# Softmax sums by one-column products in a score bank, and three moves of row splits, in an attention and expert kernel

## The chip, the cores and the metric

The kernel runs on one core of one Trainium2 chip. The metric is device time in microseconds (us). Before the change it is 1903.29 us, the median of 3 runs (1898.18 to 1903.45). The engines are called as the profile calls them: PE is TensorE, DVE is VectorE, ACT is ScalarE, POOL is GpSimd, SP is SyncE (which issues all DMAs here).

## The reference

A block of cross attention is followed by a block of routed experts. The change is in the attention. `x` has 16 batches of 56 tokens of 256 numbers, the context 16 batches of 1500 keys; there are 16 heads of 128. Cut to what matters:

```python
q = rms_norm(x @ q_w + q_b, nq_s).reshape(B, S, H, D)
k_txt = rms_norm(txt_ctx @ k_w + k_b, nkt_s)   # 1243 keys a batch
k_img = rms_norm(img_ctx @ ki_w + ki_b, nki_s) # 257 keys a batch
attn = softmax(einsum('bshd,blhd->bhsl', q, k) / sqrt(D))
out = einsum('bhsl,blhd->bshd', attn, v)       # once for text, once for image
x = x + (out_txt + out_img).reshape(B, S, INNER) @ o_w + o_b
```

The two softmaxes are separate. Each needs, for every token and head, the sum of its exponentials over its keys; the reciprocal of this sum scales the average of the values.

## The kernel before, in words

The kernel has five stages, one after the other: a prologue with a layer norm, the projection of the queries (`project`), the attention (`attend`), the outputs (`outputs`) and the experts (`experts`). `project` folds the key weights into the queries, so that `attend` multiplies the raw context with "absorbed queries" of 256 numbers per token and head, 896 columns a batch, worked on as two halves of 448 columns.

All fp32 products are made from two parts: a value is split into a high part (fp32r) and the rest, and three products (high by high, high by rest, rest by high) stand for one.

`attend` loops over 16 batches (`batches`, L951: the first, a loop, the last, and a tail). A batch has 13 tiles of up to 128 keys: tiles 0 to 2 are the image, tiles 3 to 12 the text. Tile 2 holds a single key and is called `LONE`. A unit `u` is one tile and one half, so a batch has 26 units (`UNITS`), and the code of every engine is written out as 26 steps. The order on each engine is the order of the code, with semaphores between the engines; nothing is planned at run time.

What one step does, engine by engine:

- **PE** (`body_of`, L1252): the score products of unit `step` into one of three PSUM banks (`scores`, L1178: six products of 448 columns; for the single key two products of prepared terms, L1190); at steps 3, 5 (text, of the batch before) and 9, 11 (image) two products that add up a finished sum over the partitions (`sums`, L1227, into the bank `GRAM`); on even steps five products for the norm of the next tile (`gram`, L1173); then six products of the average of unit `step - 2` (`average`, L1210; none for the single key). The averages of the last two units follow in steps 0 and 1 of the next batch (`carried`).
- **ACT** (`body`, L1373): the exponential of unit `step - 1`, twice, once as high part `p_high` and once in full into the score bank (`exponentials`, L1332); on even steps the high part of a tile two ahead (`prepare`, L1316); at some steps a high part of the absorbed queries (`split_u` at 1, 3 and 10, 12), of the single key's terms (`split_lone` at 14, 16), a copy of the finished text averages (`copy_o`), and at steps 4, 6, 10, 12 a copy of a finished sum row (`copy_sum`, L1357).
- **DVE** (`body`, L1526): `take` (L1516) of unit `step - 1`: the rest `p_low` of the exponential (`split_probs`), the add to the running sum `p_sum` (`add`, L1471; for the single key a row of one partition), and the seed, a copy of the query biases into the bank just read, which the scores three units later add onto (`seed`, L1430). On even steps `norm` (L1445), the mean square of a tile's keys; at steps 2, 4, 6, 8 and 10 it stands ahead of the `take` (`norms_first`, L1531). `split_sum` (L1483) splits a finished sum in two operations, at steps 1, 2 (text) and 7, 8 (image). `reciprocals` (L1504) at steps 10 (text) and 16 (image).
- **POOL** (`body`, L1701): on even steps `key_root` (L1628, the inverse root of the norm), on odd steps `split_tile` (`c_low`, the rest of a tile, natural and transposed, 512 numbers a partition) and `twice` (`c_twice`, an operand of the norm); beside these one longer operation in nearly every even step (`scale_u`, `split_u`, `scale_o`), and at steps 17 and 19 `split_lone`, the rest of the single key's terms.
- **SP** (`body_of`, L1081): one tile load per tile, and at certain tiles (`set_end`, L1059) the loads and stores of the batch's ends. A finished sum goes from a row in SBUF to DRAM (`store_sums`), back as columns of 112 partitions by 8 (`load_sums`), gets its reciprocal on DVE, goes to DRAM again (`store_reciprocals`) and comes back spread over all partitions (`load_reciprocals`), where POOL scales the averages (`scale_o`).

The score banks take turns by `u % 3`; unit 0 of a batch uses the bank of unit 24 of the batch before. The order of DVE around a unit:

```python
def take(it, u, has_next):
    if u // 2 == LONE:
        dve.wait_ge(exp_done, UNITS * it + u + 1 + CREDIT["exp_done"])
        seed_after(it, u, has_next)
    split_probs(it, u)
    add(it, u)
    if u // 2 != LONE and (has_next or u + SC_RING < UNITS):
        dve.wait_ge(sum_added, UNITS * it + u + 1 + CREDIT["sum_added"])
        seed_after(it, u, has_next)
```

A layer norm (`layer_norm`, L117) runs in the prologue and ahead of the experts; its L142 makes fp32 products of 112 stationary columns with one moving column. The prologue's `ones` is used there.

Of the kernel before, what the change touches and what calls it, by code (L numbers as in the profile page):

```python
# [49 lines left out]
AVERAGES = UNITS - 2  # L50
TOK = 112
# [25 lines left out]
          "sum_split": 4, "stage_used": TILES, "o_copied": 2, "recip_ready": 2, "o_scaled": 4, "norm_summed": 3,  # L77
          "lone_split": 2, "max_tile_done": 1, "sum_wide": 2, "sum_copied": 1, "max_scores": 1, "max_listed": 16, "sums_stored": 32,
# [17 lines left out]
def averaged(u):  # L96

    return u + 1 - min(max(u + 1 - 2 * LONE, 0), 2)

# [81 lines left out]
def build(nc, xT_in, ctx_in, lone_in, qw_in, kw_in, kwb_in, vw_in, small_in, router_in, bias_in, ffn_in, out):  # L181
    ctx = ExitStack()
    with ctx:
# [15 lines left out]
        with attn:  # L199
# [19 lines left out]
            with proj:  # L219
# [10 lines left out]
                spent = attend(nc, ctx_in, lone_in, qw_in, kw_in, psum, ident, minus_half, zeros, small, key_scale, *by_head,  # L230
# [189 lines left out]
def project(nc, qw_in, kw_in, psum, ident, minus_half, zeros, small, key_scale, bias_high, bias_low, x_high, x_low,  # L420
# [4 lines left out]
    with ctx:  # L425
# [112 lines left out]
        def tensor(pe):  # L538
# [262 lines left out]
def attend(nc, ctx_in, lone_in, qw_in, kw_in, psum, ident, minus_half, zeros, small, key_scale, bias_high, bias_low, x_high,  # L801
# [4 lines left out]
    with ctx:  # L806
# [18 lines left out]
        sum_cols, recip_cols = sb("sum_cols", [TOK, 2, NTOK]), sb("recip_cols", [TOK, 2, NTOK])  # L825
# [44 lines left out]
        def first_low(gp):  # L870
# [21 lines left out]
        p_sum_high, p_sum_low = sb("p_sum_high", [P, 2, HALF], F32R), sb("p_sum_low", [P, 2, HALF], F32R)  # L892
        sum_row = sb("sum_row", [1, 4, HALF])
# [13 lines left out]
        sums_dram = nc.dram_tensor("sums", [2 * B, HS], F32, kind="Internal").ap()  # L907
# [31 lines left out]
        sum_added, sum_high_ready, sum_split, sum_wide, sum_copied = (  # L939
            sem("sum_added"), sem("sum_high_ready"), sem("sum_split"), sem("sum_wide"), sem("sum_copied"))  # L940
        sums_stored, sums_loaded, recip_ready, recip_stored, recip_loaded = (
            sem("sums_stored"), sem("sums_loaded"), sem("recip_ready"), sem("recip_stored"), sem("recip_loaded"))
# [22 lines left out]
        def bank_of(u):  # L965
            return SC + u % SC_RING

# [5 lines left out]
        def _(sp):  # L973
# [24 lines left out]
            def store_sums(it, s):  # L998
                sp.wait_ge(sum_copied, 4 * it + 2 * s + 2 + CREDIT["sum_copied"])
                sp.dma_start(sums_dram[ds(2 * it + s, 1), :], sum_row[0:1, 2 * s:2 * s + 2, :]  # L1000
                             .rearrange("o a n -> o (a n)")).then_inc(sums_stored, 16)

            def load_sums(it, s):
                sp.wait_ge(sums_stored, 16 * (2 * it + s + 1) + CREDIT["sums_stored"])
                sp.wait_ge(recip_ready, 2 * it + s - 1 + CREDIT["recip_ready"])
                sp.dma_start(sum_cols[:, s, :], sums_dram[ds(2 * it + s, 1), :].rearrange("a (p i) -> p (a i)", i=NTOK))\
                    .then_inc(sums_loaded, 16)

            def store_reciprocals(it, s):
                sp.wait_ge(recip_ready, 2 * it + s + 1 + CREDIT["recip_ready"])  # L1010
                sp.dma_start(recip_dram[ds(2 * it + s, 1), :].rearrange("a (p i) -> p (a i)", i=NTOK),
                             recip_cols[:, s, :]).then_inc(recip_stored, 16)
# [105 lines left out]
            def tail(it):  # L1118
                store_o(it - 1, IMAGE)
                store_sums(it - 1, TEXT)  # L1120
                load_sums(it - 1, TEXT)
# [7 lines left out]
            sp.sem_inc(sums_stored, CREDIT["sums_stored"])  # L1129
# [24 lines left out]
        def _(pe):  # L1154
            pe.sem_inc(scores_done, CREDIT["scores_done"])
            pe.sem_inc(av_done, CREDIT["av_done"])
            pe.sem_inc(sum_wide, CREDIT["sum_wide"])
# [20 lines left out]
            def scores(it, u, safe):  # L1178
# [20 lines left out]
                if not safe:  # L1199
# [27 lines left out]
            def sums(it, s, half, grams):  # L1227

# [1110 lines left out]
```

## Time and profile before

| what | us |
|---|---|
| median of 3 runs | 1903.29 |
| lowest, highest | 1898.18, 1903.45 |
| the profiled execution | 1903.73 |
| its span, first to last instruction | 1902.0 |
| mean granted clock of TensorE | 0.971 of full |
| POOL busy | 1204.3 |
| DVE busy | 1397.3 |
| ACT busy | 985.9 |

The attention fills the span from about 233 to 1447 us. A row of the timeline gives the start, the duration, engine, line, operation, the program's names (out <- in), the shapes and how many instructions it merges; in brackets stands the idle time of the engine just before it and what ended it. Instructions on one engine overlap a little, so a start may come before the end of the one before. Matmuls are pipelined: one of 448 columns lasts 0.37 us, and the next starts some 0.2 us after it. A line can be that of a helper: L1424 is every subtraction on DVE, L1314 every plain copy on ACT.

### The profile page before, as it was taken

What the parts mean: (1) busy time and instruction counts of PE and PEld (TensorE: products, weight loads), DVE (VectorE), ACT (ScalarE), POOL (GpSimd) and SP (SyncE); (2) the same over time, 40 slices, a digit from 0 to 9 for tenths busy, and PEclk for the clock granted to TensorE, in tenths of its full rate; (3) what the DMA queues carried; (4) which work ended last, traced back from release to release, by engine and by line L of the source; (5) the groups of instructions that cost most, each with busy time, mean ns of one, the idle gap of its engine ahead of it and who ended that gap; (6) DMA issues with size and microseconds to landing.
All of it is one profiled execution on the core that took longest, in us unless ns stands there. A gap on an engine that the chain in (4) does not pass through costs nothing. (4 is left out here: it accounts for less than half of the span.)

```text
span 1902.0 us, 30825 instructions
## 1 busy us (share of the span) xinstructions
PE 1733.7 (91%) x8731; PEld 1541.6 (81%) x8731; DVE 1397.3 (73%) x2577; ACT 985.9 (52%) x1657; POOL 1204.3 (63%) x1053
## 2 busy tenths in 40 slices
PE   7899889999999999999999999999992998699998
PEld 6677778888889889888888898898891886588887
DVE  4444587887887887978878878879772664577776
ACT  3455455565555555655655565556552563244443
POOL 1333588878878888788788798798862231133332
PEclk9999899999999999999999999999996999799999
DMA  3366554566556465554565564564436782133332
GB/s 110 127 239 232 175 164 104 114 123 137 115 118 131 108 117 123 121 120 113 128 132 118 120 134 103 116 128 123 95 92 203 249 267 88 66 109 118 114 115 74
DMA packets 417365, 251.20 MB, mean 132 GB/s; under 512 B 350272, under 2 KB 368832, under 8 KB 415520
## 3 DMA queue, kind: packets, MB, share of 16 engines
q1 hardware_dynamic: 417312, 250.55, 51.5%
q8 instruction: 26, 0.43, 0.1%
q14 instruction: 27, 0.22, 0.0%
HBM read 187.71 MB, written 60.10 MB: 130 GB/s over the span
## 5 line engine op out<-in xcount | busy, mean ns | idle before, releaser
L1341 ACT ACTIVATE p_high<-psum,key_rms 128x448 fp32r<-128x448 f32 x384 | 244.8, 638 | 397.1 <-PE psum L1164 396.9
L1162 PE MATMUL psum<-p_high,c_high 128*128 128x448 f32 (+1 forms) x768 | 287.8, 375 | 48.2 <-DVE p_low L1424 48.2
L1424 DVE TENSOR_TENSOR p_low<-psum,p_high 128x448 fp32r<-128x448 f32 x384 | 236.3, 615 | 96.6 <-ACT psum L1343 95.7
L1162 PE MATMUL psum<-u_high,c_high 128*128 128x448 f32 x768 | 285.9, 372 | 20.2 <-DVE psum L1435 14.1
L1163 PE MATMUL psum<-u_low,c_high 128*128 128x448 f32 x768 | 282.9, 368 | 0.0
L1164 PE MATMUL psum<-u_high,c_low 128*128 128x448 f32 x768 | 281.8, 367 | 0.0
L1164 PE MATMUL psum<-p_high,c_low 128*128 128x448 f32 (+1 forms) x768 | 281.4, 366 | 0.0
L1163 PE MATMUL psum<-p_low,c_high 128*128 128x448 f32 (+1 forms) x768 | 281.0, 366 | 0.0
L1636 POOL TENSOR_TENSOR c_low<-stage,c_high 128x512 fp32r<-128x512 f32 x208 | 274.7, 1321 | 0.0
L1435 DVE COPY psum<-beta_wide 128x448 f32<-128x448 f32 x416 | 259.4, 627 | 20.3 <-DMA beta_wide<-absorbed_biases 4.5
L1630 POOL TENSOR_TENSOR key_rms<-key_ms,minus_half 128x1 f32<-128x1 f32 x209 | 119.4, 571 | 188.4 <-DVE key_ms L1449 183.4
L1343 ACT ACTIVATE psum<-psum,key_rms 128x448 f32<-128x448 f32 x384 | 232.5, 606 | 0.0
L1162 PEld LDWEIGHTS psum<-p_high,c_high 128*128 128x128 f32 (+1 forms) x768 | 144.0, 188 | 72.9 <-DVE p_low L1424 62.2
L1480 DVE TENSOR_TENSOR p_sum<-psum,p_sum 128x448 f32<-128x448 f32 (+1 forms) x320 | 196.2, 613 | 0.0
L1162 PEld LDWEIGHTS psum<-u_high,c_high 128*128 128x128 f32 x768 | 144.9, 189 | 44.8 <-DVE psum L1435 20.7
L2043 POOL TENSOR_TENSOR scaled_gate<-gated,p_wide 128x448 f32<-128x448 f32 x64 | 83.7, 1308 | 154.0 <-ACT gated L2144 150.5
L1649 POOL TENSOR_TENSOR c_twice<-stage,c_low 128x256 f32<-128x256 f32 x208 | 169.9, 817 | 16.4 <-POOL c_low L1636 2.4
L1449 DVE CUSTOM_DVE_ANT_0 junk<-psum,c_twice 128x257 bf16<-128x257 f32 x208 | 88.6, 426 | 92.2 <-POOL c_twice L1649 90.3
L1164 PEld LDWEIGHTS psum<-u_high,c_low 128*128 128x128 f32 x768 | 145.2, 189 | 12.7
L1163 PEld LDWEIGHTS psum<-u_low,c_high 128*128 128x128 f32 x768 | 145.2, 189 | 10.9
L1164 PEld LDWEIGHTS psum<-p_high,c_low 128*128 128x128 f32 (+1 forms) x768 | 144.1, 188 | 12.1
L1163 PEld LDWEIGHTS psum<-p_low,c_high 128*128 128x128 f32 (+1 forms) x768 | 144.3, 188 | 8.6
(245 smaller groups left out, 4077.9 us busy)
## 6 DMA issues: line engine op xcount, KB each, us to landing
stage<-in_ctx SPq DMA_DIRECT2D x210, 256.0 KB, 2.8
averages<-o_raw SPq DMA_DIRECT2D x64, 448.0 KB, 5.2
o_stage<-averages SPq DMA_DIRECT2D x32, 896.0 KB, 5.4
u_raw<-absorbed_queries SPq DMA_DIRECT2D x60, 448.0 KB, 5.5
absorbed_queries<-u_stage SPq DMA_DIRECT2D x14, 1792.0 KB, 6.8
beta_wide<-absorbed_biases SPq DMA_DIRECT2D x32, 448.0 KB, 5.3
recip_wide<-reciprocals SPq DMA_DIRECT2D x32, 448.0 KB, 4.1
p_wide<-probs_by_expert SPq DMA_DIRECT2D x32, 448.0 KB, 3.6
```

The lines of the kernel that those rows point to most:

```text
L1162: nc.tensor.matmul(out, high, rhigh, start=start, stop=False, **kw)
L1163: nc.tensor.matmul(out, high, rlow, start=False, stop=False, **kw)
L1164: return nc.tensor.matmul(out, low, rhigh, start=False, stop=stop, **kw)
L1341: nc.scalar.activation(p_high[:, probs_slot(u), :], src, ACT.Exp, scale=key_rms[:, t:t + 1])
L1343: nc.scalar.activation(out, src, ACT.Exp, scale=key_rms[:, t:t + 1]).then_inc(exp_done, 1)
L1424: return nc.vector.tensor_tensor(out, a, b, ALU.subtract)
L1435: nc.vector.tensor_copy(psum[:, bank_of(u), 0:HALF], beta_wide[:, s, cols_of(half)])\
L1449: nc.vector.tensor_tensor_reduce(out=junk[:, :], in0=psum[:, GRAM, 0:DIM + 1], in1=c_twice[:, slot(t, TWICE_RING), :], scale=1.0 / INNER, ...
L1480: added = nc.vector.tensor_tensor(total, part, total, ALU.add)
L1630: nc.gpsimd.tensor_tensor(key_rms[:, t:t + 1], key_ms[:, t:t + 1], minus_half[:, 0:1], ALU.pow)\
L1636: nc.gpsimd.tensor_tensor(c_low[:, k, :], stage[:, st, :], c_high[:, k, :].bitcast(F32), ALU.subtract)\
L1649: nc.gpsimd.tensor_tensor(c_twice[:, slot(t, TWICE_RING), 0:DIM], stage[:, st, nat], c_low[:, k, nat].bitcast(F32), ALU.add).then_inc(stag ...
```

## The change

- The sums over the partitions are made by eight fp32 products per softmax, each with 112 columns of `p_sum` as the stationary operand, every fourth one of a half's 448, and one column of ones as the moving one. They land as a block of 112 partitions by 8, in the free end of a score bank (columns 448 to 455), which DVE clears ahead of the seed. PE issues them inside `scores`, after the products of step 2 (text, of the batch before) and step 8 (image), and before the signal that the scores are done.
- The split of the sums on DVE, the old products, ACT's copies of the sum rows, and SP's stores and loads of sums are gone. DVE takes the reciprocal straight from the bank, inside `take` of units 2 and 8, ahead of the seed.
- The single key's exponentials are no longer added to `p_sum`. SP copies them from their row as 112 by 4, twice, after unit 5's exponential, and DVE adds them ahead of the image's reciprocal. ACT waits for the copies of the batch before ahead of the single key's exponential.
- `norms_first` holds at step 6 alone.
- ACT's `split_u` of the image moves from steps 10, 12 to 11, 13, its `split_lone` from 14, 16 to 15, 17; POOL's `split_lone` moves from 17, 19 to 18, 20.
- POOL's `split_tile` of the single key's tile works on the natural half alone.
- In the tail, DVE clears the block, PE makes the last text sums after the last average, and DVE takes the reciprocal.
- Three products in `project` that mark the score banks as written are 512 columns wide in place of 448.

```diff
-                nc.tensor.matmul(psum[:, b, 0:HALF], q_high[:, 0, 0:P], q_high[:, 0, 0:HALF], start=True, stop=True)\
+                nc.tensor.matmul(psum[:, b, :], q_high[:, 0, 0:P], q_high[:, 0, 0:512], start=True, stop=True)\
...
-        TEXT_SPLIT, IMAGE_SPLIT = (1, 3), (10, 12)
-        LONE_TERMS, LONE_HIGH, LONE_LOW = (12, 14), (14, 16), (17, 19)
-        TEXT_SUM_SPLIT, TEXT_SUMS, TEXT_RECIP = (1, 2), (3, 5), 10
-        IMAGE_SUM_SPLIT, IMAGE_SUMS, IMAGE_RECIP = (7, 8), (9, 11), 16
+        TEXT_SPLIT, IMAGE_SPLIT = (1, 3), (11, 13)
+        LONE_TERMS, LONE_HIGH, LONE_LOW = (12, 14), (15, 17), (18, 20)
+        TEXT_SUMS, IMAGE_SUMS = 2, 8
...
+        def sums_of(s):
+
+            return psum[0:TOK, bank_of((IMAGE_SUMS, TEXT_SUMS)[s]), HALF:HALF + NTOK]
...
+            def list_lone(it):
+                sp.wait_ge(exp_done, UNITS * it + 2 * LONE + 2 + CREDIT["exp_done"])
+                for half in range(2):
+                    sp.dma_start(lone_cols[:, NTOK // 2 * half:NTOK // 2 * (half + 1)],
+                                 lone_probs[0:1, half, :].rearrange("o (p i) -> o p i", i=NTOK // 2))\
+                        .then_inc(lone_listed, 16)
...
+                if has_prev and t == 4:
+                    store_reciprocals(it - 1, TEXT)
                 if has_prev and t == 5:
-                    store_sums(it - 1, TEXT)
-                if has_prev and t == 6:
-                    load_sums(it - 1, TEXT)
-                if has_prev and t == 8:
-                    store_reciprocals(it - 1, TEXT)
-                if has_prev and t == 9:
                     load_reciprocals(it - 1, TEXT)
                 if has_prev and t == 12:
                     store_o(it - 1, TEXT)
+                if t == 4:
+                    list_lone(it)
+                if t == 7:
+                    store_reciprocals(it, IMAGE)
                 if t == 8:
-                    store_sums(it, IMAGE)
-                if t == 9:
-                    load_sums(it, IMAGE)
-                if t == 10:
-                    store_reciprocals(it, IMAGE)
-                if t == 11:
                     load_reciprocals(it, IMAGE)
...
+                if u == TEXT_SUMS and has_prev:
+                    last = sums(it - 1, TEXT)
+                if u == IMAGE_SUMS:
+                    last = sums(it, IMAGE)
                 last.then_inc(scores_done, 1)
...
+            def sums(it, s):
+                last = 2 * (LONE if s == 0 else TILES) - 1
+                pe.wait_ge(sum_added, ADDS * it + added(last) + CREDIT["sum_added"])
+                for half in range(2):
+                    parts = p_sum[:, 2 * s + half, :].rearrange("p (n i) -> p i n", i=NTOK // 2)
+                    for i in range(NTOK // 2):
+                        at = NTOK // 2 * half + i
+                        done = nc.tensor.matmul(sums_of(s)[:, at:at + 1], parts[:, i, :], ones[:, 0:1], start=False,
+                                                stop=True, skip_group_check=True)
+                return done
...
             def tail(it):
-                for step in range(TEXT_SUMS[1] + 1):
+                for step in range(2):
                     carried(it, step)
-                    text_sums(it, step, TILES * it + 1)
+                pe.wait_ge(last_zeroed, 1)
+                sums(it - 1, TEXT).then_inc(last_sums, 1)
...
+                elif half == 0:
+                    act.wait_ge(lone_listed, 32 * it + CREDIT["lone_listed"])
...
+                if u in (TEXT_SUMS, IMAGE_SUMS):
+                    nc.vector.memset(psum[0:TOK, bank_of(u), HALF:HALF + NTOK], 0.0)
...
+                if t == LONE:
+                    return
...
             def reciprocals(it, s):
-                m = 2 * it + s
-                dve.wait_ge(sums_loaded, 16 * (m + 1))
+                m, sums = 2 * it + s, sums_of(s)
+                if s == 0:
+                    dve.wait_ge(lone_listed, 32 * (it + 1) + CREDIT["lone_listed"])
+                    nc.vector.tensor_tensor(sum_cols[:, :], sums, lone_cols[:, :], ALU.add).then_inc(lone_counted, 1)
+                    dve.wait_ge(lone_counted, it + 1)
+                    sums = sum_cols[:, :]
                 dve.wait_ge(recip_stored, 16 * (m - 1) + CREDIT["recip_stored"])
-                nc.vector.reciprocal(recip_cols[:, s, :], sum_cols[:, s, :]).then_inc(recip_ready, 1)
+                nc.vector.reciprocal(recip_cols[:, s, :], sums).then_inc(recip_ready, 1)
...
                 add(it, u)
+                if u == TEXT_SUMS and has_prev:
+                    reciprocals(it - 1, TEXT)
+                if u == IMAGE_SUMS:
+                    reciprocals(it, IMAGE)
...
-                    norms_first = step % 2 == 0 and (step + 1 in TEXT_SUMS + IMAGE_SUMS or step == 2 * LONE + 2)
+                    norms_first = step == 2 * LONE + 2
...
-                k, st = slot(t, CTX_RING), slot(t, STAGE_RING)
+                k, st, cols = slot(t, CTX_RING), slot(t, STAGE_RING), slice(DIM if t == LONE else 0, 2 * DIM)
```

## Rows read from the trace of the kernel before

**Rows 1.** Part 1 of the page: busy time, share of the span and instructions of each engine.

```profile
PE 1733.7 (91%) x8731; PEld 1541.6 (81%) x8731; DVE 1397.3 (73%) x2577; ACT 985.9 (52%) x1657; POOL 1204.3 (63%) x1053
```

**Rows 2.** Timeline of PE, batch 7: S0, its norm products, A24, the next S0.

```profile
681.20 0.37 PE L1162 MATMUL psum<-u_high,c_high 128*128 128x448 f32 x1
...
682.44 0.28 PE L1169 MATMUL psum<-gram_high,c_high 128*128 128x258 f32 x1
...
683.04 0.36 PE L1162 MATMUL psum<-p_high,c_high 91*128 91x448 f32 x1
...
755.66 0.37 PE L1162 MATMUL psum<-u_high,c_high 128*128 128x448 f32 x1
```

**Rows 3.** Timeline of PE, batch 7: first products of A2, S8, A8 and S12.

```profile
695.36 0.48 PE L1162 MATMUL psum<-p_high,c_high 128*128 128x448 f32 x1 [1.43 <-DVE p_low L1424]
...
702.96 0.47 PE L1162 MATMUL psum<-u_high,c_high 128*128 128x448 f32 x1 [0.94 <-DVE psum L1435]
...
712.95 0.47 PE L1162 MATMUL psum<-p_high,c_high 128*128 128x448 f32 x1 [1.25 <-DVE p_low L1424]
...
717.13 0.37 PE L1162 MATMUL psum<-u_high,c_high 128*128 128x448 f32 x1
```

**Rows 4.** Timeline of DVE, batch 7, from step 6 to the end of step 8.

```profile
701.93 0.43 DVE L1449 CUSTOM_DVE_ANT_0 junk<-psum,c_twice 128x257 bf16<-128x257 f32 x1 [0.64 <-POOL c_twice L1649]
...
702.29 0.62 DVE L1435 COPY psum<-beta_wide 128x448 f32<-128x448 f32 x1
702.82 1.26 DVE L1466 SCALAR_TENSOR_TENSOR o_raw<-lone_probs,lone_row,psum 128x448 f32<-128x448 f32 x2
704.00 0.74 DVE L1480 TENSOR_TENSOR p_sum<-lone_probs,p_sum 1x448 f32<-1x448 f32 x1
704.66 0.60 DVE L1424 TENSOR_TENSOR p_low<-psum,p_high 128x448 fp32r<-128x448 f32 x1
...
706.37 0.38 DVE L1488 CAST p_sum_high<-p_sum 128x448 fp32r<-128x448 f32 x1
...
710.76 1.59 DVE L1424 TENSOR_TENSOR p_sum_low<-p_sum,p_sum_high 128x448 fp32r<-128x448 f32 x1
```

**Rows 5.** Timeline of POOL, batch 7: `key_root` of steps 12, 22 and 24, one `split_lone`.

```profile
720.06 0.70 POOL L1630 TENSOR_TENSOR key_rms<-key_ms,minus_half 128x1 f32<-128x1 f32 x1 [0.84 <-DVE key_ms L1449]
...
736.08 1.17 POOL L1686 TENSOR_TENSOR x_high<-lone_terms,x_high 128x448 fp32r<-128x448 f32 x1
...
748.35 0.55 POOL L1630 TENSOR_TENSOR key_rms<-key_ms,minus_half 128x1 f32<-128x1 f32 x1 [0.55 <-DVE key_ms L1449]
...
753.62 0.55 POOL L1630 TENSOR_TENSOR key_rms<-key_ms,minus_half 128x1 f32<-128x1 f32 x1 [0.55 <-DVE key_ms L1449]
```

**Rows 6.** Timeline of DVE, end of batch 7: norm in step 24, the next S0's seed.

```profile
753.11 0.43 DVE L1449 CUSTOM_DVE_ANT_0 junk<-psum,c_twice 128x257 bf16<-128x257 f32 x1 [0.83 <-POOL c_twice L1649]
...
754.64 0.63 DVE L1435 COPY psum<-beta_wide 128x448 f32<-128x448 f32 x1
```

**Rows 7.** Timeline of PE: one-column fp32 products of the two layer norms.

```profile
18.25 3.21 PE L142 MATMUL psum<-ones,ln_square 128*112 128x1 f32 x32
...
1607.95 5.76 PE L142 MATMUL psum<-ones,ln_square 128*112 128x1 f32 x30 [0.63 <-ACT ln_square L171]
```

**Rows 8.** Timeline of the attention's end, PE and DVE.

```profile
1427.28 0.37 PE L1233 MATMUL psum<-p_sum_high,ones_r 128*128 128x448 f32 x1
...
1433.00 0.20 DVE L1508 RECIPROCAL recip_cols<-sum_cols 112x8 f32<-112x8 f32 x1 [4.96 <-DMA sum_cols<-sums]
```

**Rows 9.** Timeline of ACT, batch 7: the exponential of unit 1.

```profile
688.55 0.63 ACT L1343 ACTIVATE psum<-psum,key_rms 128x448 f32<-128x448 f32 x1
```

**Rows 10.** Stretches: busy us (instructions) of PE, PEld, DVE, ACT, POOL; clock, DMA share, GB/s.

```profile
23.38:26.79 3.41, 3.41 (x18) 3.41 (x17) 1.58 (x15) 0.64 (x1) 1.02 (x1) 0.50 0.45 147
247.70:250.50 2.80, 0.17 (x1) 0.00 (x0) 0.98 (x4) 0.96 (x2) 2.06 (x3) 1.00 1.03 405
252.07:255.48 3.41, 3.41 (x13) 3.12 (x13) 2.49 (x5) 1.76 (x3) 2.83 (x3) 0.50 0.61 247
```

More of the change, by code:

```diff
@@ L1176, in gram, with scores @@
                 gram_products(slot(t, CTX_RING), int(t >= IMG_TILES)).then_inc(gram_done, 1)
-            def scores(it, u, safe):
+            def scores(it, u, safe, has_prev):
                 t, half = divmod(u, 2)
@@ L1225, in average @@
                 last.then_inc(av_done, 1)
-            def sums(it, s, half, grams):
-                n = 4 * it + 2 * s + half
-                pe.wait_ge(sum_split, n + 1 + CREDIT["sum_split"])
-                pe.wait_ge(sum_copied, n + CREDIT["sum_copied"])
-                pe.wait_ge(norm_summed, grams + CREDIT["norm_summed"])
-                nc.tensor.matmul(psum[:, GRAM, 0:HALF], ones_r[:, :], p_sum_high[:, half, :], start=True, stop=False)
-                nc.tensor.matmul(psum[:, GRAM, 0:HALF], ones_r[:, :], p_sum_low[:, half, :], start=False, stop=True)\
-                    .then_inc(sum_wide, 1)
+            def sums(it, s):
[8 more added lines that the diff above has]
+                return done
             def carried(it, step):
@@ L1240, in carried @@
                     average(it - 1, UNITS - 2 + step)
-            def text_sums(it, step, grams):
-                if step in TEXT_SUMS:
-                    sums(it - 1, TEXT, TEXT_SUMS.index(step), grams)
-            def sums_left(it, step, has_prev):
-                if (has_prev and step - 1 in TEXT_SUMS) or step - 1 in IMAGE_SUMS:
-                    issued = len([x for x in TEXT_SUMS + IMAGE_SUMS if x < step])
-                    pe.wait_ge(sum_copied, 4 * it - 2 + issued + CREDIT["sum_copied"])
             def body_of(safe):
@@ L1254, in body @@
                     for step in range(UNITS):
-                        scores(it, step, safe)
-                        grams = TILES * it + step // 2 + 2
-                        if has_prev:
-                            text_sums(it, step, grams)
-                        if step in IMAGE_SUMS:
-                            sums(it, IMAGE, IMAGE_SUMS.index(step), grams)
+                        scores(it, step, safe, has_prev)
                         if step % 2 == 0:
-                            sums_left(it, step, has_prev)
                             gram(*ahead(it, step // 2 + 1))
@@ L1367, in carried @@
                     copy_o(it - 1, step - 1)
-            def text_sums(it, step):
-                if step - 1 in TEXT_SUMS:
-                    copy_sum(it - 1, TEXT, TEXT_SUMS.index(step - 1))
             def body(it, has_prev, has_next):
@@ L1394, in tail @@
             def tail(it):
-                for step in range(TEXT_SUMS[1] + 2):
+                for step in range(3):
                     carried(it, step)
-                    text_sums(it, step)
             def maxima(it):
@@ L1504, in reciprocals, with take @@
             def reciprocals(it, s):
-                m = 2 * it + s
-                dve.wait_ge(sums_loaded, 16 * (m + 1))
-                dve.wait_ge(recip_stored, 16 * (m - 1) + CREDIT["recip_stored"])
-                nc.vector.reciprocal(recip_cols[:, s, :], sum_cols[:, s, :]).then_inc(recip_ready, 1)
-            def carried(it, step):
-                if step in TEXT_SUM_SPLIT:
-                    split_sum(it - 1, TEXT, TEXT_SUM_SPLIT.index(step))
-                if step == TEXT_RECIP:
-                    reciprocals(it - 1, TEXT)
-            def take(it, u, has_next):
+                m, sums = 2 * it + s, sums_of(s)
[4 more added lines that the diff above has]
+                    sums = sum_cols[:, :]
+                dve.wait_ge(recip_stored, 16 * (m - 1) + CREDIT["recip_stored"])
+                nc.vector.reciprocal(recip_cols[:, s, :], sums).then_inc(recip_ready, 1)
+            def take(it, u, has_prev, has_next):
                 if u // 2 == LONE:
@@ L1528, in body @@
                     if has_prev and step == 0:
[L1529 to L1531 removed]
+                        take(it - 1, UNITS - 1, True, True)
+                    norms_first = step == 2 * LONE + 2
                     if norms_first:
@@ L1534, in body @@
                     if step >= 1:
-                        take(it, step - 1, has_next)
+                        take(it, step - 1, has_prev, has_next)
                     if step % 2 == 0 and not norms_first:
                         norm(*ahead(it, step // 2 + 1))
-                    if has_prev:
-                        carried(it, step)
-                    if step in IMAGE_SUM_SPLIT:
-                        split_sum(it, IMAGE, IMAGE_SUM_SPLIT.index(step))
-                    if step == IMAGE_RECIP:
-                        reciprocals(it, IMAGE)
                     if has_next and step in LONE_TERMS:
@@ L1547, in tail @@
             def tail(it):
-                take(it - 1, UNITS - 1, False)
-                for step in range(TEXT_RECIP + 1):
-                    carried(it, step)
+                take(it - 1, UNITS - 1, True, False)
+                nc.vector.memset(sums_of(TEXT), 0.0).then_inc(last_zeroed, 1)
+                dve.wait_ge(last_sums, 1)
+                reciprocals(it - 1, TEXT)
             def maxima(it):
```

78 lines of the change are left out of this document (22 added, 56 removed).

## The prediction

> **What bounds the kernel now.** I read the page first: TensorE (PE) is busy 91% of the span [rows 1]. That makes PE's own order the first suspect, so I took the timeline of batch 7. S8 means the score products of step 8, A8 the average of unit 8; a step is scores, on even steps five norm products, and an average. S0 starts at 681.20 and the next S0 at 755.66: a batch is 74.46 us [rows 2]. The same rows price PE at full clock: six score products 1.24 (0.2 each), five norm products 0.60; six of an average are as many as of the scores, 1.22 to 1.24. So the reader can tell which step is longer than its work.
>
> The waits of PE are in three places [rows 3]: A2 for `p_low` (1.43), S8 for its seed (0.94), A8 for `p_low` (1.25). Idle time is counted there from a product's end, 0.17 after the next could have started, so they cost 1.6, 1.1 and 1.4. Two have one cause: VectorE (DVE) has the split of a finished sum ahead of the `p_low`; half 1's split of the image sums ends at 712.35 [rows 4], PE's wait right after it. S8's wait is of another kind: the norm of tile 4 at 701.93 waits for POOL's (GpSimd's) `c_twice`, and the seed of unit 8 stands behind that norm on DVE [rows 4].
>
> That leads to a second chain, nearly as long as PE's. POOL goes from `key_root` to the next `key_root` in 5.27, with its wait for the norm (0.55) inside [rows 5]; two steps of PE are 2x1.24 + 2x1.22 + 0.60 = 5.5. At the batch's end the norm at 753.11 stands on DVE ahead of the `p_low`, the add and the seed (754.64) that the next S0 needs [rows 6]. A seed that starts at 702.29 frees its scores at 702.96 [rows 3, 4], 0.67 later; so S0 could start at 755.31 and starts at 755.66. PE sets the batch now, and the chain through POOL is 0.35 behind it.
>
> **The change on PE's path.** Eight products of 448 columns a batch go (steps 3, 5, 9, 11): 8x0.2 = 1.6. Ahead of the signal of S2 and again of S8 come eight fp32 products of one column each. A layer norm has this form (112 stationary columns, one moving): 16 products, which the trace shows as 32 records, in 3.21 us [rows 7], 0.10 a record, so 1.6 us for eight products. But there the stationary columns lie side by side; here they are every fourth fp32 of a row, and no row shows weights read so. Lower bound: 0.10. Upper bound, by the nearest row of a slower load: the same products at half clock, 30 records in 5.76 us, 0.19 [rows 7], as if each column took two cycles; 3.0 for eight. I take 0.10, the row of the same shape and clock, and keep 0.19 for the range.
>
> DVE loses the eight operations of the sum splits and the two adds of the single key; it gains two clears, two reciprocals and one add, all of 112x8, some 0.2 each by the reciprocal of that shape [rows 8]; the clear in front of a seed I take at 0.12, an estimate below that. The waits of A2 and A8 go. What is late next is S8. In the new order the norm of step 2 stands behind `take` of unit 1. The exponential of unit 1 ends at 688.55 + 0.63 = 689.2 [rows 9]; a take (`p_low`, add, seed) is 706.37 - 704.66 = 1.71 [rows 4]; so this norm is at 690.9. Two turns of POOL from there, 5.24 each (5.27 less what DVE's accumulator read puts in), give the norm of tile 4 at 701.4, the seed 0.36 + 0.12 later, at 701.9, and S8 at 702.55: 0.4 earlier than now. PE would be there at 702.96 - 1.1 - 1.6 - 0.8 + 1.6 = 701.0 (its two waits and four old sum products go, the text sums come). So the text sums are covered by a wait of 1.5 at S8; without that cover they would cost 1.6 a batch.
>
> From S8 to S12 PE then has four scores, four averages, two norm groups and the image sums: 4x1.24 + 4x1.22 + 1.2 + 1.6 = 12.6, so S12 is at 715.1; it is at 717.13 now [rows 3]. Gain on PE's path: 2.0.
>
> **The change on POOL's chain.** The norm of tile 5 comes behind seed 8 (0.53), two `o_raw` (1.18) and two takes (2x1.71) [rows 4], at 707.0. Two more turns and the 0.5 from norm to `key_root` put the `key_root` of step 12 at 718.0; it is at 720.06 now, and from there to 753.62 it is 33.56 [rows 5]. In this stretch the single key's two splits (1.17 each) move from odd to even steps. Now each stands between `c_twice` and `key_root` and so covers the wait for the norm; then it stands behind `key_root` and covers nothing: 2x0.55 more, 1.2 with the gaps between starts. So step 24's `key_root` is at 718.0 + 33.56 + 1.2 = 752.75, 0.87 earlier than now, and S0 is free at 755.31 - 0.87 = 754.44. PE alone would be there at 715.1 + 38.53 (755.66 - 717.13) = 753.65. The batch becomes 73.24, a gain of 1.22: POOL's chain is the bound, and 0.8 of PE's gain stays unused.
>
> **The end.** The last sum product of half 0 starts at 1427.28 and the last reciprocal at 1433.00, behind two copies, a store and a load [rows 8]. Then it is 1.6 of products and 0.2 to the reciprocal, 1429.1: 3.9 less.
>
> **The clock.** It fell to 1.2 GHz at 23.38, shortly after the one-column products of the first layer norm, and at 252.07, after 2.80 us in which PE worked 0.17; PE was then busy without a break and the clock was back 3.41 us later [rows 7, 10]. In the new batch a wait of 1.5, S8 and 1.6 of one-column products stand in a row. I expect a fall in about half of the batches, an estimate by likeness to those two places. A score product is 0.2 apart at full clock and 0.37 at half (scaled as the records of rows 7, 0.19 to 0.10), so 3.41 us at half clock cost 1.55; POOL's chain hides 0.8 of it. 8x0.75 = 6.
>
> **At nothing.** ScalarE's four copies go and its row splits move by a step: it is busy 52% of the span [rows 1], and what it waits for is PE. The half split saves POOL some 0.6 ahead of `c_twice` of tile 2, but the norm that reads this comes at 690.9 by DVE, so nothing follows. SP: two stores and two loads of sums a batch go, two small copies come. At tile 4 SP now stands until the single key's exponentials are over (by PE's order at about 697.5), with the load of tile 7 queued behind, whose slot is free only with tile 4's `c_twice` at 701.4. New waits: ScalarE's, on copies of the batch before; PE's, on the image's last add (done at 695, needed at 703.8); DVE's, on the copied row (issued at 698, needed at 708), with the seed of S11 behind it, needed at 712.7. Three start products become 64 columns wider, once.
>
> **The sum**, against the profiled execution's 1903.73 (span 1902.0 and 1.7 around it; the median of the runs is 0.44 lower): 15x1.22 + 1 for the first batch (an estimate: it has the image sums alone) + 3.9 - 6 = 17. Forecast 1886.5; with no fall of the clock 1880.5.
>
> **Rivals.** *The weight load at a stride* (slower). If a column takes two cycles, the eight products take 3.0, 1.44 more than counted. At step 2: S3 starts at 691.4, its exponentials end 2.6 later (1.24 of products, 0.2 to their end, two activations of 0.6), the take at 695.7, and POOL's `c_twice` is there at 696.1: only 0.4 is in hand, so S8 moves by 1.0. At step 8 all of the 1.44 is on PE's path. S0 is at 753.65 + 2.44 = 756.1, 0.4 later than now: 7 us, less 2.5 gained at the end, 1908. With one-column stretches twice as long I would expect a fall in most batches and nothing that hides it, up to 16x1.55 more, 1933; the middle is 1920. It decides from 0.17 a record. For it: no row has such a load. Against it: a layer norm's load at half clock is the only one that slow. By the Trainium skill, "SBUF — State Buffer", section Specifications, a line of SBUF has 16 bytes and full bandwidth needs at least two hits in each; here every column is on a line of its own, so that rule speaks against this change and would give 1920. No run here shows it yet.
>
> *No fall of the clock* (1880.5). For it: the waits of rows 3 left the clock of batch 7 at full.
>
> *POOL's chain gives nothing.* The 0.87 that S0 gains over 755.31 is a difference of two larger things, 2.06 earlier at step 12 and 1.2 lost on the single key's splits. If the turns of POOL in steps 2 to 12 take together 0.9 more than 5.24 each, it is gone, and the batch is 74.1 or more: 1894 to 1900, from the end and a remnant. For it: that sum rests on turns of the batch's end; against it: DVE's copies of the sums, which ran beside POOL there, are gone.
>
> **How the numbers follow.** Chances: forecast 0.38, no fall 0.22, POOL gives nothing 0.14, strided load 0.26. About 0.3%, 5.7 us, can be told from no change. Faster has the first two and a little of the third: 0.62; same 0.12; slower 0.26. The likeliest case alone reaches from 1878 to 1893. The range starts at 1872, PE's gain of 2.0 a batch with POOL's chain shorter than counted and some falls, and goes to 1918, the lower half of the strided case.
>
> **What would show it.** Right: new records at 0.10; no wait at A2 and A8; the longest wait of a batch at S8, for its seed; S0 released by a seed behind a norm that waits for `c_twice`; batches of 73.2 to 74.0; the last reciprocal 1.8 after the last average; a granted clock under 1.00 behind S8 in some batches. Wrong: records at 0.17 or more; a wait at S2 to S4; batches of 72.5 (POOL's chain is no bound) or 74.4.

## The result, and the profile after

The changed kernel takes 1962.62 us, the median of four runs (1962.13 to 1989.63), beside 1901.76 us before (four runs): the ratio is 1.0356, 95% interval 1.0289 to 1.0423. It is slower by 3.6%, and 45 us above the range. The profiled execution took 1962.13 us, with a span of 1960.3, 58.3 more than before.

Part 1 of the page of the changed kernel [rows 1]: PE has more work, DVE less.

```profile
PE 1831.5 (93%) x9115; PEld 1659.1 (85%) x9115; DVE 1263.0 (64%) x2466; ACT 967.4 (49%) x1593; POOL 1173.8 (60%) x1053
```

The timeline of PE in batch 7 of the changed kernel: S0, the text sums, A2, S8, the image sums, the norm products behind them, A8, S12 and the next S0 [rows 2, 3].

```profile
701.78 0.47 PE L1156 MATMUL psum<-u_high,c_high 128*128 128x448 f32 x1 [0.35 <-DVE psum L1406]
...
708.60 3.26 PE L1232 MATMUL psum<-ones,p_sum 128*112 128x1 f32 x16
711.72 0.37 PE L1163 MATMUL psum<-gram_high,c_high 128*128 128x258 f32 x1
...
717.09 0.37 PE L1156 MATMUL psum<-p_high,c_high 128*128 128x448 f32 x1
...
724.41 0.47 PE L1156 MATMUL psum<-u_high,c_high 128*128 128x448 f32 x1 [1.28 <-DVE psum L1406]
...
725.74 3.26 PE L1232 MATMUL psum<-ones,p_sum 128*112 128x1 f32 x16
728.86 0.56 PE L1163 MATMUL psum<-gram_high,c_high 128*128 128x258 f32 x1
...
737.52 0.37 PE L1156 MATMUL psum<-p_high,c_high 128*128 128x448 f32 x1
...
741.18 0.37 PE L1156 MATMUL psum<-u_high,c_high 128*128 128x448 f32 x1
...
780.29 0.48 PE L1156 MATMUL psum<-u_high,c_high 128*128 128x448 f32 x1 [0.57 <-DVE psum L1406]
```

Three things are to be seen. The 16 records of a sum (eight products, two records each) take 3.12 us (708.60 to 711.72), 0.195 a record, where 32 records of the same shape took 3.21 [rows 7]. A2 and A8 no longer wait. And behind the image sums a product takes longer for a while than the same one earlier (0.56 where 0.37 stood).

The third is the clock. Stretches of the same batch, with the columns of [rows 10]: the text sums, the wait at S8, S8 with the image sums, and what follows.

```profile
708.60:711.80 3.20, 3.20 (x18) 3.20 (x17) 2.18 (x4) 1.78 (x4) 0.94 (x3) 1.00 1.10 235
720.60:724.40 3.80, 2.53 (x15) 2.05 (x13) 1.03 (x5) 2.45 (x6) 3.17 (x4) 1.00 0.03 1
724.40:727.54 3.14, 3.13 (x16) 3.06 (x16) 3.10 (x6) 0.53 (x1) 2.02 (x3) 1.00 0.68 230
727.54:734.37 6.83, 6.83 (x25) 6.35 (x25) 3.69 (x10) 1.13 (x2) 3.41 (x3) 0.50 0.44 106
734.37:741.00 6.63, 6.63 (x37) 6.18 (x36) 4.00 (x8) 4.53 (x8) 3.82 (x5) 1.00 0.33 83
```

At 727.54, within the image sums, the clock falls to 1.2 GHz and is back at 2.4 GHz 6.83 us later. All 15 batches behind the first have this fall at the same place and as long; before, no batch between 255.48 and 1433 had one. The batch is 780.29 - 701.78 = 78.51 us, 4.05 more than before [rows 2]; from the second on all are between 78.39 and 78.56. From the first S0 to the last one it is 58.2 us more than before, so the batches hold the whole loss.

What follows on DVE in batch 7 (norm and seed ahead of S8, then the norm of step 8), and at the attention's end on PE and DVE [rows 4, 8]:

```profile
723.37 0.43 DVE L1420 CUSTOM_DVE_ANT_0 junk<-psum,c_twice 128x257 bf16<-128x257 f32 x1 [3.11 <-POOL c_twice L1608]
...
723.74 0.61 DVE L1406 COPY psum<-beta_wide 128x448 f32<-128x448 f32 x1
...
730.44 0.43 DVE L1420 CUSTOM_DVE_ANT_0 junk<-psum,c_twice 128x257 bf16<-128x257 f32 x1 [1.48 <-PE psum L1165]
...
1488.79 3.26 PE L1232 MATMUL psum<-ones,p_sum 128*112 128x1 f32 x16
...
1492.09 0.21 DVE L1474 RECIPROCAL recip_cols<-psum 112x8 f32<-112x8 f32 x1 [4.39 <-PE psum L1232]
```

### The profile page after: what moved, and what is told of

It reads as the page before. It is cut to its first block and busy times, and to the rows that moved or that the text cites. A ratio compares the mean times of both kernels' runs of the same rounds, so it can differ in the third digit from the quotient of the medians.

```text
span 1960.3 us, 31227 instructions
## 1 busy us (share of the span) xinstructions
PE 1831.5 (93%) x9115; PEld 1659.1 (85%) x9115; DVE 1263.0 (64%) x2466; ACT 967.4 (49%) x1593; POOL 1173.8 (60%) x1053
## 5 line engine op out<-in xcount | busy, mean ns | idle before, releaser
L1156 PE MATMUL psum<-u_high,c_high 128*128 128x448 f32 x768 | 292.6, 381 | 35.4 <-DVE psum L1406 27.1
L1157 PE MATMUL psum<-u_low,c_high 128*128 128x448 f32 x768 | 288.2, 375 | 0.0
L1158 PE MATMUL psum<-p_high,c_low 128*128 128x448 f32 (+1 forms) x768 | 288.0, 375 | 0.0
L1157 PE MATMUL psum<-p_low,c_high 128*128 128x448 f32 (+1 forms) x768 | 287.4, 374 | 0.0
L1595 POOL TENSOR_TENSOR c_low<-stage,c_high 128x512 fp32r<-128x512 f32 (+1 forms) x208 | 260.5, 1252 | 0.0
L1608 POOL TENSOR_TENSOR c_twice<-stage,c_low 128x256 f32<-128x256 f32 x208 | 152.9, 735 | 16.3 <-POOL c_low L1595 2.4
L1157 PEld LDWEIGHTS psum<-u_low,c_high 128*128 128x128 f32 x768 | 149.5, 195 | 12.2
L1158 PEld LDWEIGHTS psum<-p_high,c_low 128*128 128x128 f32 (+1 forms) x768 | 148.7, 194 | 13.1
L1156 PEld LDWEIGHTS psum<-p_high,c_high 128*128 128x128 f32 (+1 forms) x768 | 149.6, 195 | 9.9
L1157 PEld LDWEIGHTS psum<-p_low,c_high 128*128 128x128 f32 (+1 forms) x768 | 149.1, 194 | 9.5
```

The source lines that it names most:

```text
L1156: nc.tensor.matmul(out, high, rhigh, start=start, stop=False, **kw)
L1157: nc.tensor.matmul(out, high, rlow, start=False, stop=False, **kw)
L1158: return nc.tensor.matmul(out, low, rhigh, start=False, stop=stop, **kw)
L1595: nc.gpsimd.tensor_tensor(c_low[:, k, cols], stage[:, st, cols], c_high[:, k, cols].bitcast(F32), ALU.subtract).then_inc(ctx_low, 1)
L1608: nc.gpsimd.tensor_tensor(c_twice[:, slot(t, TWICE_RING), 0:DIM], stage[:, st, nat], c_low[:, k, nat].bitcast(F32), ALU.add).then_inc(stag ...
```

## The experiments

**Columns side by side, and every second one.** The stationary columns are read `STEP` fp32 apart: 4 in the changed kernel, 1 and 2 here; the two transfers on SP that must match, the copies of the single key's row and the store of the reciprocals, are cut into shorter pieces.

```diff
-                    parts = p_sum[:, 2 * s + half, :].rearrange("p (n i) -> p i n", i=NTOK // 2)
+                    parts = p_sum[:, 2 * s + half, :].rearrange("p (g n i) -> p g i n", n=TOK, i=STEP)
...
-                        done = nc.tensor.matmul(sums_of(s)[:, at:at + 1], parts[:, i, :], ones[:, 0:1], start=False,
+                        done = nc.tensor.matmul(sums_of(s)[:, at:at + 1], parts[:, i // STEP, i % STEP, :], ones[:, 0:1], start=False,
```

> The changed kernel with one thing altered: the 112 stationary columns of each one-column product lie side by side in p_sum instead of every fourth fp32 (the reciprocals and the single key's row are then stored and copied in pieces of 4 bytes). Theory (the stride doubles the weight load): the records of the sums are 0.10 us apart instead of 0.195, PE loses 1.5 us less at step 2 and at step 8, and the fall of the clock behind step 8 becomes rarer or goes; a batch is 73.2 to 74.0 us against 78.5, the time 1880 to 1890. Rival A (fp32 products are that slow between fp32r products, whatever the stride): the records stay at 0.19, the time within 5 us of the changed kernel's, 1962. Rival B (the fall of the clock is caused by the one-column products as such): records at 0.10, the clock still falls once a batch for 6.8 us, 1925 to 1940.

> As the run with columns side by side, but every second fp32 (a stride of 8 bytes, pieces of 8 bytes in the copies). If a line of 16 bytes has to be hit twice for full speed, as the Trainium skill, SBUF - State Buffer, section Specifications, states, two columns share a line and the records are 0.10 apart, the time equal to that of side by side within 5 us. If any stride halves the load, 0.19 and 1955 to 1965. If the load slows in proportion to the lines touched, 0.12 to 0.15 and a time between.

Side by side: 1907.79 us, 1.0025 (1.0015 to 1.0035). Every second: 1904.94 us, 1.0010 (0.9997 to 1.0023). The text sums of batch 7, first side by side (with the image sums of the same batch below them), then every second column:

```profile
684.44 1.64 PE L1234 MATMUL psum<-ones,p_sum 128*112 128x1 f32 x16
...
700.32 2.03 PE L1234 MATMUL psum<-ones,p_sum 128*112 128x1 f32 x16
```

```profile
687.96 1.72 PE L1234 MATMUL psum<-ones,p_sum 128*112 128x1 f32 x16
```

Starts are 0.094 and 0.10 apart, half of the 0.195 at every fourth column: the distance of the columns is the price. The weight loads (PEld) of the same sums show it too, first in the changed kernel, then side by side:

```profile
708.40 3.38 PEld L1232 LDWEIGHTS psum<-ones,p_sum 128*112 128x112 f32 x16
```

```profile
684.24 1.75 PEld L1234 LDWEIGHTS psum<-ones,p_sum 128*112 128x112 f32 x16
```

By the Trainium skill, "SBUF — State Buffer", section Specifications, a 16-byte line wants two hits for full bandwidth; the three runs (four, two and one column in a line) agree.

One thing sets the strided load apart from a slower clock, with which the prediction compared it. Side by side the image sums take 2.03 us where the text sums take 1.64, because the clock falls in them at 701.40. In the changed kernel it falls in the image sums too, at 727.54, and they take the same 3.26 us as the text sums at full clock: at 16 bytes the steps are 0.206 at either level of the clock.

The records came as the theory had them, the time did not: 1880 to 1890 were expected, because the falls were to become rare. They came in 8 of the 15 batches behind the first. Three S0 of the run side by side, a batch without a fall between the first two and one with a fall of 6.83 us between the last two (with its S8); and two of its stretches at 0.50:

```profile
604.37 0.47 PE L1158 MATMUL psum<-u_high,c_high 128*128 128x448 f32 x1 [0.39 <-DVE psum L1408]
...
677.61 0.48 PE L1158 MATMUL psum<-u_high,c_high 128*128 128x448 f32 x1 [0.53 <-DVE psum L1408]
...
699.00 0.47 PE L1158 MATMUL psum<-u_high,c_high 128*128 128x448 f32 x1 [1.56 <-DVE psum L1408]
...
753.86 0.47 PE L1158 MATMUL psum<-u_high,c_high 128*128 128x448 f32 x1 [0.39 <-DVE psum L1408]
```

```profile
701.40:708.23 6.83, 6.83 (x24) 6.30 (x24) 4.43 (x11) 1.14 (x3) 3.85 (x4) 0.50 0.82 194
851.59:855.00 3.41, 3.41 (x13) 3.11 (x12) 3.09 (x10) 1.13 (x2) 1.53 (x2) 0.50 0.83 276
```

So a batch is 73.24 without a fall, 76.25 with the long one, and 74.7 with the short one. This takes the 4.05 apart: a gain of 1.22 (74.46 to 73.24), 3.01 for the fall (76.25 - 73.24), and what is left, 78.51 - 76.25 = 2.26, for the strided load. The border between the last two is not sharp, since a fall does not slow the strided sums in it: three batches of the next run, strided and without a fall, take 76.0, which would give 2.8 to the load and 2.5 to the fall.

**The image sums later.** In the changed kernel, strided as it is, they go from step 8, behind a wait, to step 14, where PE has none.

```diff
-        TEXT_SUMS, IMAGE_SUMS = 2, 8
+        TEXT_SUMS, IMAGE_SUMS = 2, 14
```

> The changed kernel with its strided columns, but the image sums at step 14 instead of 8, away from PE's wait for S8 (their reciprocals are stored and loaded three tiles later). Theory (the clock falls where a wait and a one-column stretch stand close together): no fall behind step 8 nor behind step 14; a batch is shorter by the 3.1 us that the fall cost, 75.4, the time about 1915. Rival (3 us of one-column products alone make the clock fall): one fall a batch of 6.8 us behind step 14, and the time stays at 1955 to 1965.

1970.13 us, 1.0347 (1.0326 to 1.0368) beside before: no better than the changed kernel, and nearer the rival's 1955 to 1965 than the theory's 1915. Of the 15 batches behind the first ten had two falls (six of them two of 3.41 us), two had one, and three had none. Ahead of and in the falls of one batch, behind the text sums and behind the image sums:

```profile
713.80:717.90 4.10, 4.10 (x24) 4.08 (x24) 2.21 (x4) 2.44 (x6) 0.98 (x3) 1.00 1.20 252
717.92:721.33 3.41, 3.41 (x11) 3.01 (x10) 2.25 (x6) 1.36 (x2) 2.85 (x3) 0.50 0.73 160
749.00:752.05 3.05, 3.05 (x17) 3.05 (x16) 2.23 (x4) 0.00 (x0) 2.76 (x3) 1.00 0.00 1
752.05:755.46 3.41, 3.41 (x13) 3.20 (x13) 1.69 (x5) 1.62 (x3) 1.21 (x2) 0.50 0.49 154
```

PE counts as busy in all of the 4.10 and 3.05 us ahead of these falls; there is no wait. So a fall can come behind 3.1 us of one-column products alone. It need not: three batches here have none, and the text sums of the changed kernel, as long, are never followed by one. What decides it stays open.

**The row splits back.** Side by side, with ACT's and POOL's splits at their old steps.

```diff
-        TEXT_SPLIT, IMAGE_SPLIT = (1, 3), (11, 13)
-        LONE_TERMS, LONE_HIGH, LONE_LOW = (12, 14), (15, 17), (18, 20)
+        TEXT_SPLIT, IMAGE_SPLIT = (1, 3), (10, 12)
+        LONE_TERMS, LONE_HIGH, LONE_LOW = (12, 14), (14, 16), (17, 19)
```

> Columns side by side, and ScalarE's row splits and GpSimd's splits of the single key back at the steps of the kernel before (image split 10, 12; single key 14, 16 on ScalarE, 17, 19 on GpSimd). Theory (the chain through GpSimd's key_root bounds S0, and moving the single key's splits behind key_root costs it 1.2 us a batch): a batch 0.8 us shorter than with columns side by side alone, 10 to 13 us less in all. Rival (PE's own order bounds the batch): within 3 us of the run with columns side by side.

1894.68 us, 0.9962 (0.9948 to 0.9976). Two S0 with a batch without a fall between them:

```profile
675.01 0.37 PE L1158 MATMUL psum<-u_high,c_high 128*128 128x448 f32 x1
...
747.51 0.37 PE L1158 MATMUL psum<-u_high,c_high 128*128 128x448 f32 x1
```

S0 waits for no seed now, and the batch is 72.50 where it was 73.24: moving the splits cost 0.74 a batch. ScalarE's splits and POOL's went back together, but POOL's own rows show the cost: three of its turns around the two single-key splits, side by side first, then with the splits back:

```profile
652.56 0.55 POOL L1591 TENSOR_TENSOR key_rms<-key_ms,minus_half 128x1 f32<-128x1 f32 x1 [0.55 <-DVE key_ms L1422]
...
670.66 0.55 POOL L1591 TENSOR_TENSOR key_rms<-key_ms,minus_half 128x1 f32<-128x1 f32 x1 [0.55 <-DVE key_ms L1422]
```

```profile
723.11 0.55 POOL L1591 TENSOR_TENSOR key_rms<-key_ms,minus_half 128x1 f32<-128x1 f32 x1 [0.55 <-DVE key_ms L1422]
...
740.02 0.55 POOL L1591 TENSOR_TENSOR key_rms<-key_ms,minus_half 128x1 f32<-128x1 f32 x1 [0.55 <-DVE key_ms L1422]
```

They take 18.10 and 16.91: 1.19 more where the splits stand behind `key_root`, as forecast (1.2). Falls came in 6 of the 15 batches.

**The norm first, at steps 2 and 6.** On top of the last kernel, `norms_first = step in (2, 6)`.

> Side by side, the row splits back at their old steps, and at steps 2 and 6 the norm of a tile ahead of the take on VectorE, so that the c_twice and the seed of S8 come earlier. Theory W (the wait at S8 and the one-column products behind it fall together to the clock): the wait at S8 shrinks from about 1.4 us by up to 1.0, the falls behind the image sums go or become fewer than in the run with the splits back (there about half of the batches), batches 72.5 with few exceptions, 1872 to 1888 us. Rival C (the one-column products alone do it): as many falls as before and 1890 to 1896 us, with the batches that have none at 72.5 because PE and not POOL's chain sets them.

1883.49 us, 0.9895 (0.9868 to 0.9922). S8 moved by 0.1 only (its wait is 1.49 us), so the edit did not do what I meant it to, though the time is in the range of theory W. The profiled execution, at 1896.55 the slowest of the five, still has falls in 6 of the 15 batches, as the kernel without the edit; its mean clock is 0.958, and the runs down to 1878.92 have 0.963 to 0.966. Batches without a fall take 72.33 to 72.44. Whether a small shift of S8 makes falls rarer is not shown.

**Between the score products.** The eight products of a sum no longer stand in a row: one or two go ahead of each of the six score products of the step. First with the columns side by side and the splits back, then in the changed kernel.

```diff
+                for n in range(2 if between else 0):
+                    next(between)
                 nc.tensor.matmul(out, high, rhigh, start=start, stop=False, **kw)
+                if between:
+                    next(between)
                 nc.tensor.matmul(out, high, rlow, start=False, stop=False, **kw)
+                if between:
+                    next(between)
                 return nc.tensor.matmul(out, low, rhigh, start=False, stop=stop, **kw)
```

> Side by side, splits back, and the eight one-column products of a sum each stand between two score products of steps 2 and 8 instead of in a row behind them. Theory (both W and C, since no stretch of one-column products is left): no fall of the clock in any batch after the first, every batch at most 72.5, 1866 to 1872 us. If their weight loads hide behind the score products' 448 columns, a sum costs under 1.0 us instead of 1.5, and a batch is 71.5 to 72.2 where PE sets it. Rival (the falls come with the change of data type or with fp32 products anywhere in a busy stretch): falls in about half of the batches as before, 1885 to 1896 us.

> The changed kernel as it is, strided loads and all, but the eight products stand between the score products. If the 62 us are clock and load together: no falls (3.1 us a batch back), and the batches are 78.5 - 3.1 = 75.4 if the strided load still takes 0.195 a record beside other products, so about 1917 us. If the load hides behind the 448 columns of the score product ahead of it, the batch is POOL's chain, 73.2 to 73.6, about 1884 us. If falls go on: 1950 to 1963 us.

A miss twice: 1903.03 us, 0.9995 (0.9978 to 1.0013), and 1964.13 us, 1.0331 (1.0300 to 1.0362). The start of step 8 in the first one, a batch without a fall:

```profile
777.70 0.55 PE L1241 MATMUL psum<-ones,p_sum 128*112 128x1 f32 x4 [1.63 <-DVE psum L1414]
778.11 0.45 PE L1160 MATMUL psum<-u_high,c_high 128*128 128x448 f32 x1
778.40 0.27 PE L1241 MATMUL psum<-ones,p_sum 128*112 128x1 f32 x2
778.52 0.45 PE L1163 MATMUL psum<-u_low,c_high 128*128 128x448 f32 x1
778.81 0.27 PE L1241 MATMUL psum<-ones,p_sum 128*112 128x1 f32 x2
```

From one score product to the next it is 0.41, the 0.2 of a score product and the 0.2 of a sum product: nothing of the short load hides behind 448 columns. In the second kernel, with the strided columns, the same distance is 0.52 where 0.2 and 0.39 would make 0.59: some 0.07 of it hides:

```profile
628.77 0.45 PE L1158 MATMUL psum<-u_high,c_high 128*128 128x448 f32 x1
629.06 0.37 PE L1239 MATMUL psum<-ones,p_sum 128*112 128x1 f32 x2
629.29 0.45 PE L1161 MATMUL psum<-u_low,c_high 128*128 128x448 f32 x1
```

The falls stayed, in 10 of the 15 batches of the first kernel and in all of the second (77.9 to 79.6 a batch). Mixing other products in does not keep the clock.

**Short and later.** Both edits that had failed or not been enough alone: columns side by side (1.5 us a sum), splits back, and the image sums at step 14.

> Side by side, splits back, the image sums at step 14, where no wait of PE stands near them, instead of step 8. Theory W (a wait beside 1.5 us of one-column products is needed): no falls behind the image sums, batches 72.5, 1866 to 1876 us. Rival C (1.5 us of them are enough by themselves in some phase): falls in about half of the batches again, some behind the text sums and some behind the image sums, 1885 to 1900 us.

1876.70 us, 0.9867 (0.9843 to 0.9890). S8's wait, the image sums, what follows them, and the next whole batch:

```profile
689.70:693.00 3.30, 1.73 (x9) 1.28 (x8) 2.24 (x6) 1.68 (x3) 2.67 (x4) 1.00 0.09 1
709.40:711.20 1.80, 1.80 (x19) 1.75 (x18) 1.74 (x4) 0.30 (x1) 1.80 (x2) 1.00 0.06 20
711.20:718.00 6.80, 6.80 (x39) 6.36 (x39) 5.67 (x13) 4.32 (x8) 6.09 (x6) 1.00 0.30 78
743.00:815.40 72.40, 70.83 (x390) 65.73 (x389) 52.59 (x113) 41.93 (x72) 60.62 (x55) 1.00 0.64 124
```

Batches 2 to 15 have no fall; each is 72.40 to 72.47. The wait at S8 is still there (1.57 us), and so are the sums; only apart. The last batch has a fall of 3.41 us, and it is not behind sums: it starts at S8, right behind a wait of 1.77 us. Its wait and its fall:

```profile
1342.50:1344.40 1.90, 0.17 (x1) 0.20 (x2) 1.29 (x4) 1.67 (x3) 1.24 (x3) 1.00 0.09 1
1344.42:1347.83 3.41, 3.41 (x12) 3.14 (x12) 3.38 (x7) 1.13 (x2) 1.74 (x2) 0.50 0.69 45
```

So 1.5 us of one-column products were followed by falls where they stood behind a wait of some 1.5 us (in 6 to 10 of 15 batches), and in no batch behind the first where they stood away from one; behind 3.1 us of them falls came away from a wait too.

**All together.** Every second column, splits back, image sums at step 14, the norm first at steps 2 and 6.

> All that the runs pointed to, in one kernel: two neighbouring columns a line (every second fp32), the row splits at their old steps, the image sums at step 14, the norm ahead of the take at steps 2 and 6. Theory (PE's order with no fall of the clock sets the batch): no falls after the first batch, batches of 72.3 to 72.5, 1868 to 1878 us, within 0.3% of the run with contiguous columns and the image sums at step 14 (1876.7), since the norm's place was worth 0.13 a batch. Rival (the two extra pieces per line or the earlier norm bring the falls back): 1885 us or more.

1872.41 us, 0.9851 (0.9831 to 0.9871), with no fall in any batch behind the first: 1.5% faster than before, where the changed kernel is 3.6% slower. The earlier norm added nothing that shows: batches are 72.44 to 72.56.

## Why the prediction was wrong

**The step that failed** is the price of the new products: "I take 0.10, the row of the same shape and clock". The row had columns side by side; the products here have them 16 bytes apart and take 0.195, the upper bound that I kept for the range [rows 7]: a sum of eight products takes 3.12 us, not 1.6. It was the only thing about the new operation that no row showed, and I chose by shape rather than by what was different. The load alone turns a gain of 1.22 a batch into a loss of 1.0 to 1.6. The strided rival was right in this, with a chance of 0.26; the range, which ended at 1918, left the upper half of it out. "As if each column took two cycles" is not what the trace shows: two cycles would take twice as long at half the clock, and the steps stay as they are. That the bound came near the measured 0.195 is luck in part.

**The second step that failed** is the price of the clock, "8x0.75 = 6". With the load as forecast, the run side by side is still no faster than before (1.0025), and in the changed kernel the falls cost some 2.5 to 3.0 in each of 15 batches, about as much as the load.

**The rival's own time** was too low (1920, at most 1933) by both of its terms. For the load it gave S8 1.0 and step 8 1.44, and the batch 1.66 more than the forecast (756.1 - 754.44). S8 came 22.63 us behind S0 where the run side by side has 21.39, 1.24 more, and the image sums take 1.6 more; less the 0.74 that POOL's chain leaves PE to spare, that is 2.1, and 2.3 to 2.8 was measured. For the clock it priced a fall at 1.55, and each fall of the changed kernel costs 2.5 to 3.0, being twice as long.

**The clock.** With short loads, falls came in 8 of the 15 batches behind the first, as forecast. Their price was wrong twice. Half of them lasted 6.83 us, not 3.41 [rows 10]. And "POOL's chain hides 0.8 of it" failed: a short fall costs 74.7 - 73.24 = 1.5, nearly the whole 1.55. POOL's `key_root` of step 10 shows why, in a batch without a fall and in the one with the fall at 851.59:

```profile
635.96 0.55 POOL L1591 TENSOR_TENSOR key_rms<-key_ms,minus_half 128x1 f32<-128x1 f32 x1 [0.55 <-DVE key_ms L1422]
```

```profile
859.91 0.55 POOL L1591 TENSOR_TENSOR key_rms<-key_ms,minus_half 128x1 f32<-128x1 f32 x1 [1.75 <-DVE key_ms L1422]
```

It starts 31.59 and 32.77 us behind S0 (604.37 and 827.14): it waits 1.2 longer for the norm, and the norm waits for PE's own norm products, which the fall has delayed (as at 730.44 above). The chain is late with PE and hides nothing. Eight falls cost some 18 us instead of 6.

**What held**, read from the runs without the stride: no wait at A2 and A8; S8 21.35 to 21.39 behind S0 in most batches (forecast 21.35), released by a seed behind a norm that waits for `c_twice`; S12 at 34.04 where no fall lies ahead of it (33.9); the batch at 73.24 (73.24) with S0 waiting for its seed; and 72.50 (72.45) for PE alone with the splits back, so 0.74 of the 0.8 that POOL's chain was to eat is shown. The last reciprocal started 1.89 behind the last product of the averages (1.8).

**What else was off**, by the run side by side, which is the forecast's own case (1886.5) and took 1901.98 in the profile, its fastest run. The falls are 12 of the difference. The first batch was to gain 1 and lost 1.8 (75.95 to 77.76), with a clock fall of 10.24 us in it where 3.41 stood before. The gain of 3.9 at the end came (5.93 to 1.89 from last average to reciprocal) but was gone at the span's end: from that reciprocal on it is 472.84 us, and 468.95 before. Against these, the first S0 came 3.9 earlier than before (229.21 and 233.10), for which the forecast had no reason. The output stage begins with the clock at 0.50 for 37.55 us where it was 30.72 before. In the kept executions of all runs the time from the last reciprocal on goes with this stretch: 468.25 to 471.27 us with 30.72 (three runs), 470.77 to 472.84 with 34.13 (four), 472.84 to 478.74 with 37.55 (four). That the one causes the other was not tried.

## What to carry to other kernels

A row prices a new operation only if it reads its operands the same way: look at the address step of the stationary operand, not only at its shape; here steps of 4 and 8 bytes were cheap and 16 bytes cost double. One-column products did not always hold TensorE's clock here, however busy the profile calls the engine in them: keep such a stretch short and away from the waits of TensorE, and price a fall in full, because a chain that waits for TensorE's own products hid none of it. Before a helper's splits are moved to other steps, see whether they covered a wait where they stood.

## What was not expected of the hardware

- The one-column fp32 products, paced by their weight loads: 0.094 us a record with stationary columns 4 bytes apart, 0.10 at 8, 0.195 at 16. Those at 16 took as long when the clock was at 0.50.
- The clock fell in stretches in which PE and its weight loads were busy with hardly a gap (4.10 and 4.08 of 4.10 us), when three quarters of that time were one-column products.
- A one-column product with columns side by side costs its full 0.2 between two products of 448 columns; with columns 16 bytes apart it costs 0.32 there, and 0.39 in a row.
